# One more pass of count products in layers 1 to 3 of a graph network, and another placing of layer 0's chunk counts

## The reference

```python
edge_index = jnp.stack([src, dst])
# layer 0: hypercomplex message, gate and degree norm, summed at the destination
m = clifford_linear(h_src * r_uv, msg_w, msg_b) * gate * norm
h_out = clifford_linear(h_hc + segment_sum(m, dst), upd_w, upd_b)
x = _layernorm(x + h_out)
# layers 1 to 3: mean over the neighbours, two products
def _sage_conv(x, src, dst, Wl, bl, Wr, n):
    return _mean_aggregate(x, src, dst, n) @ Wl.T + bl + x @ Wr.T
h = relu(_sage_conv(x, src, dst, W1l, b1l, W1r, n))
h = relu(_sage_conv(h, src, dst, W2l, b2l, W2r, n))
x = _layernorm(x + _sage_conv(h, src, dst, W2l, b2l, W2r, n))
```

## Time and profile before

| | us |
|---|---|
| median of 3 runs | 3838.79 |
| lowest and highest run | 3831.48, 3844.26 |
| span of the profiled execution | 3293.7 |
| setup | about 170 |
| layer 0 | about 1397 |
| layers 1, 2, 3 | about 573, 570, 584 |

### The profile page before, as it was taken

How to read it: one execution, slowest core, us unless ns; L and a number is a source line. 1 busy time by engine, 2 the same in 40 slices (tenths; PEclk the granted TensorE clock), 3 DMA queues, 4 the chain that set the end, 5 groups by cost and what they waited for, 6 DMA issues and landing times. The chain is left out here.

```text
span 3293.7 us, 54777 instructions
## 1 busy us (share of the span) xinstructions
PE 2864.3 (87%) x16731; PEld 2464.3 (75%) x16731; DVE 2458.8 (75%) x5529; ACT 2224.0 (68%) x3945; POOL 2351.4 (71%) x2185
## 2 busy tenths in 40 slices
PE   6559999999999989997599999669999957999985
PEld 4448877787778878786488888558888846888884
DVE  7968888888888888887466667546666745787786
ACT  1057777777777777774577877468877836777771
POOL 6267777777777777773577777567777756777773
PEclk6579999999999999998799999889999978999997
DMA  4256666665556666663766666376666647666662
GB/s 136 73 133 168 173 165 167 167 167 165 167 164 168 165 173 167 168 169 113 228 196 201 199 194 188 105 246 207 201 195 197 184 134 225 204 210 205 206 185 89
DMA packets 335600, 573.59 MB, mean 174 GB/s; under 512 B 47029, under 2 KB 231686, under 8 KB 335302
## 3 DMA queue, kind: packets, MB, share of 16 engines
q0 software_dynamic: 101088, 277.97, 30.4%
q1 hardware_dynamic: 230697, 289.55, 28.1%
q10 hardware_dynamic: 3517, 2.48, 0.3%
HBM read 491.85 MB, written 77.97 MB: 173 GB/s over the span
## 5 line engine op out<-in xcount | busy, mean ns | idle before, releaser
L1483 POOL DMA_INDIRECT rows_arena<-table_h,src_idx x1128 | 1236.6, 1096 | 483.8 <-issue 364.0
L2052 PE MATMUL bank<-wide_counts,h_pairs 128*128 128x512 f32 (+1 forms) x4116 | 945.7, 384 | 123.6 <-ACT wide_counts L1632 104.0
L1483 POOL DMA_INDIRECT rows_arena<-table_scaled_x,src_idx x782 | 839.0, 1073 | 285.8 <-issue 273.6
L2052 PEld LDWEIGHTS bank<-wide_counts,h_pairs 128*128 128x128 f32 x4116 | 735.4, 193 | 262.9 <-issue 128.3
L1989 PE MATMUL bank<-rel_pairs,ftype_hot 125*128 125x258 f32 x4688 | 711.0, 299 | 51.3 <-ACT ftype_hot L1610 51.0
L1989 PEld LDWEIGHTS bank<-rel_pairs,ftype_hot 125*128 125x128 f32 x4688 | 620.6, 191 | 85.5 <-ACT ftype_hot L1610 51.1
L1632 ACT CAST wide_counts<-rows_arena 128x1024 fp32r<-128x1024 bf16 (+1 forms) x525 | 549.8, 1047 | 68.0 <-DMA rows_arena<-edge_counts 67.9
L1832 DVE TENSOR_TENSOR h_pairs<-rows_arena,h_pairs 128x512 fp32r<-128x512 f32 (+1 forms) x525 | 352.9, 682 | 259.6 <-ACT h_pairs L1629 254.9
L1824 DVE TENSOR_TENSOR row_pairs<-rows_arena,row_pairs 128x1024 fp32r<-128x1024 f32 x282 | 343.1, 1218 | 208.8 <-ACT row_pairs L1619 202.5
L1629 ACT CAST h_pairs<-rows_arena 128x512 fp32r<-128x512 f32 (+1 forms) x525 | 320.9, 611 | 197.3 <-PE bank L2052 152.9
L1653 ACT CAST rows_arena<-bank 128x448 bf16<-128x448 f32 (+1 forms) x812 | 368.3, 505 | 119.3 <-PE bank L2038 74.9
(11 more groups left out here) (186 smaller groups left out, 3098.9 us busy)
## 6 DMA issues: line engine op xcount, KB each, us to landing
rows_arena<-edge_counts SPq DMA_DIRECT2D x234, 512.0 KB, 4.0
edge_counts<-fcount SPq DMA_DIRECT2D x52, 832.0 KB, 6.3
rows_arena<-in_edge_type_dram SPq DMA_DIRECT2D x195, 187.5 KB
rows_arena<-table_h SPq DMA_DIRECT2D x36, 512.0 KB, 11.9
rows_arena<-table_h,src_idx POOLq DMA_INDIRECT x1128, 3.6
rows_arena<-table_scaled_x,src_idx POOLq DMA_INDIRECT x782
table_h<-chunk_info SPq DMA_DIRECT2D x96, 128.0 KB, 4.0
rows_arena<-edge_counts SPq DMA_DIRECT2D x39, 256.0 KB, 3.1
```

Of the source, the lines that this page charges most:

```text
L1483: pool.indirect_dma_start(out=rows[:, g % ring, c, :], out_offset=None, in_=table[:, :], in_offset=bass.IndirectOffsetOnAxis(ap=src_idx[:, ...
L2052: last = pe.matmul(bank[2 + h][:, 0:cols_of(w)], h_pairs[:, v % HALVES, part, b % HALF, h * P:(h + 1) * P], wide_counts[:, v % HALVES, b % ...
```

## The change

```diff
-PASSES, PASS_COLS, LAST_COLS = 7, 512, 256
+PASSES, PASS_COLS, LAST_COLS = 8, 512, 256
...
             def counts_at(position):
-                return [i for i in range(ND if first else 0) if i * 2 * NG // ND == position]
+                quad = [i for i in range(ND if first else 0) if i * NG // ND == position // 2]
+                return quad[-1:] if position % 2 else quad[:-1]
```

## The result

The kernel after took 3785.67 us (median of 4 runs, 3774.07 to 3796.82), the kernel before 3841.53 us on the same occasion (4 runs). The ratio is 0.9845, interval 0.9807 to 0.9884: the change makes the kernel faster by 1.5%. The prediction said slower, 4045 us.

What follows compares the result with a forecast made beforehand. The prediction took DVE to bound layer 0 and PE layers 1 to 3; 106 + 25 + 25 + 32 + 1 = 189 us on the 3293.7 us span became a 4045 us median, range 3930 to 4150 us.

Steps and rivals of the forecast that it cites:

- From the span to the median: Whole kernel: timed runs lie 545 us above the span; adding 189 us gives 4028 or 4059 us, middle 4045.
- The sum for the profiled execution: Whole kernel: 106 + 25 + 25 + 32 + 1 = 189 us, on a span of 3293.7 us.
- layers 1 and 2: The eighth pass adds 44.9 us on PE, sixteen quads less remove 16.5 us: +25 us for each layer.
- layer 3: The same +25 us, and seven node blocks moved to the end, -13 and +20 us: +32 us.
- Layer 0's term: 64 more counts at 1.52 us each on DVE, 97 us, and eight more clears, 9 us: +106 us.
- The placing: Layer 0: two products in a row in 78 quads, hidden in DVE's slot; rival that 40 to 90 us surface, 15 in 100.
- The signs: Profile after: DVE waiting tens of us for relation products means the placing shows; shorter layers 1 to 3 mean gathers led.
- PE as the bound of layers 1 to 3: PE is busy for 451.3 of 461 us in layer 1's main stretch, so added matmuls cost time there.
- The end of layer 3: 16 node blocks come after the last quad, where 9 did; DVE takes 2.91 us each, 20 us more.
- the gathers were the pace: Rival, layers 1 to 3: POOL's gathers set the pace, 90 us go from each layer, some 3660 us; 7 in 100.
- Its own threshold: The rival that gathers set the pace decides from the point where each of layers 1 to 3 gains over 35 us.
- The rule on weight loads: Layers 1 to 3: by the weight loads' busy share PE has 16% to spare, room for all 49 added units; not followed.

Runs made afterwards that it cites:

- experiment 1: The kernel before, unchanged, profiled anew on a pausing chip: 3785.52 us, span 3785.9 us.
- the first profile: The profiled execution of the kernel before that the prediction read: span 3293.7 us, with no pauses.
- experiment 2: The kernel after, unchanged, on the same pausing chip as experiment 1: 3736.01 us, ratio 0.9887 to the kernel before.
- experiment 9: The kernel after, unchanged, on a quiet chip: 3505.29 us against 3297.95 us for the kernel before, ratio 1.0621.
- experiment 3: Kernel before with layer 0 counting eight passes, layers 1 to 3 still seven passes and 94 quads: 3814.3 us, ratio 1.0069, pausing chip.
- experiment 6: Kernel before with eight passes of dense products in layers 1 to 3, still 94 quads: 3418.18 us, ratio 1.0379, quiet chip.
- experiment 7: Kernel before with only 78 of 94 quads in layers 1 to 3, still seven passes: 3239.97 us, ratio 0.9837, quiet chip.
- experiment 10: The kernel of experiment 6 again, beside the kernel before on another quiet chip: 3414.62 us, ratio 1.0342.
- experiment 17: Kernel before with two of four row gathers left out from the fifth quad on in all four layers: 3228.94 us, ratio 0.8555, pausing chip.
- experiment 15: Kernel before with plain transfers replacing two of four gathers from the fifth quad on in layers 1 to 3: 3534.24 us, ratio 0.9388, pausing chip.
- experiment 16: Kernel before with 18 short POOL clears replacing two of four gathers from each fifth-on quad, layers 1 to 3: 3513.72 us, ratio 0.9326, pausing chip.
- experiment 5: Kernel before with two of four gathers left out from the fifth quad on in layers 1 to 3: 3234.85 us, ratio 0.9822, quiet chip.
- experiment 12: The kernel of experiment 6 on a pausing chip: 3906.46 us, ratio 1.0142 to the kernel before.
- experiment 13: The kernel of experiment 7 on a pausing chip: 3646.29 us, ratio 0.9463 to the kernel before.
- experiment 11: The kernel of experiment 5 on a pausing chip: 3533.08 us, ratio 0.9161 to the kernel before.
- experiment 4: Kernel before with eight passes and 78 quads in layers 1 to 3, layer 0 still counting seven: 3686.85 us, ratio 0.9756, pausing chip.
- experiment 8: Kernel after with a wait and 60 PE register additions behind 17 quads in each of layers 1 to 3: 3520.53 us, ratio 1.0692, quiet chip.
- experiment 18: Kernel after with two of four row gathers left out from the fifth quad on in all four layers: 3466.58 us, ratio 0.9179, pausing chip.

## Why the prediction was wrong

- **"From the span to the median" failed.** The prediction saw that the timed runs lay 545 us above the span and carried its sum over in two ways, as a fixed part or as a factor of 1.166, with 4045 us in the middle. The runs showed that a gap of this size is pauses in layers 0 to 3, and that these answer to the change: on one pausing chip 490 us before (experiment 1, 492 us over the first profile's span) and 233 us after (experiment 2). It named the gap, built on the stages of an execution that had none of it, and took for granted that the change would leave it alone or stretch it. "No row says what that is" was right, and should have widened the range to a gain; it was 7 in 100.
- **The sum for the profiled execution was right.** 189 us forecast, 204 us in the windows of experiment 9, +207 us by its times. By terms: layer 0 106 forecast and 121 measured, layers 1 and 2 25 each and 16 and 19 measured, layer 3 32 and 48.
- **Layer 0's term.** On a quiet chip DVE sets the pace and each count costs it 1.9 us (121/64), a little over the 1.52 us and the clears. On a pausing chip DVE is busy for 71% of the layer (1195.54 of 1678), the pauses of PE set the pace, and the same counts cost 38 us (experiment 3).
- **The placing** was hidden, as said. PE now waits for ACT's staging 103 times and 114.7 us on the quiet chip, against 26.0, but DVE's waits for relation products grew to 5.6 us only. How much of the 15 us by which layer 0 exceeded its term is the placing isn't known. With seven passes the old and the new rule put all 406 counts in the same places, so the placing has no effect apart from the eighth pass. With 470 counts the old rule too would put three into 78 quads, 38 of them with two at the second place; it wasn't tried.
- **The signs** misled in the pausing condition. DVE waited for relation products by tens of us in the kernel after (68.0 us, and 61.2 "remote"), which was to mean that the placing shows; but the kernel before has 52.3 and 107.7 us of the same waits in experiment 1, with the old placing.
- **PE as the bound of layers 1 to 3** is shown for a quiet chip by experiments 6, 7 and 10: +126 and +117 us for a pass, -52 us for 16 quads. The end of layer 3 was undersized: with eight passes and 94 quads it takes 636 us (experiment 6), with 78 quads 637 us, so the quads taken away give nothing back there.
- **The rival "the gathers were the pace"** had the right instruction and the wrong mechanism. On a quiet chip POOL isn't the pace. On a pausing chip nothing waits for them for long either; PE's pauses come with them. Its own threshold (each layer gains over 35 us) was met in layer 2 only.
- **The rule on weight loads** (the Trainium skill, "Perfetto Trace Analysis", Identifying the Most-Contended Engine) would have given room for the pass. The quiet runs don't bear it out: the layer grew although PEld was busy for 452.79 of 582 us.

How the pauses go with the gathers, by windows of the same work on both kinds of chip (where the quiet side has no such run, experiment 17 takes layer 0 of before and experiments 15 and 16 take experiment 5). POOL's share is its busy time over the layer's, on the quiet chip where there is a run, else in the run itself:

| layer | gathers, per us on the quiet chip | POOL busy | quiet, pausing (us) | longer by |
|---|---|---|---|---|
| before, 0 | 978, 0.70 | 75% | 1397, 1678 | 20% |
| before, 1 | 376, 0.66 | 73% | 566, 627 | 11% |
| after, 0 | 978, 0.64 | 71% | 1518, 1715 | 13% |
| experiments 6 and 12, 1 | 376, 0.63 | 67% | 601, 659 | 10% |
| experiments 7 and 13, 1 | 312, 0.58 | 61% | 540, 567 | 5% |
| experiment 15, 1 | 196, 0.36 | 60% | 542, 552 | 2% |
| after, 1 | 312, 0.54 | 57% | 582, 596 | 2% |
| experiment 16, 1 | 196, 0.36 | 54% | 542, 544 | 0% |
| experiment 17, 0 (quiet: as before) | 596, 0.43 | 50% | 1397, 1393 | 0% |
| experiments 5 and 11, 1 | 196, 0.36 | 40% | 542, 546 | 1% |

The eighth pass takes 64 gathers out of each layer and makes the layer longer, and the counts make layer 0 longer for the same gathers; both lower the rate, and POOL's share with it. That one of the two is what matters is read from this table and not shown, and they aren't told apart: the loss follows POOL's share about as well as the rate. The rows come from several chips, and layer 3 of experiment 13 doesn't fit (623 us against 575, 8%, at 0.54 per us).

## What to carry to other kernels

Compare the span of the profiled execution with the timed runs before pricing anything on it: if they differ by more than the timed runs do among themselves, the profile may be of another condition, and the terms read from it may have the wrong sign. Price a change against both conditions where waits "remote" or clock falls show that there are two. In this kernel, on a pausing chip, trading gathers for matmuls won 89 us in layers 1 to 3 (experiment 4), though PE seldom waits for a gather and the same trade costs time on a quiet chip.

## What the runs showed of the hardware

- The same program takes 3292 to 3298 us on some chips and 3766 to 3852 us on others, with a spread of up to 1.4% between the runs on one chip. The records number the chips: 5 and 13 paused, 2 was quiet, and number 0 was quiet in experiments 5 to 8 and paused in 15 to 18. Whether that was one device in two conditions or two devices isn't known.
- On a pausing chip the engines that wait for PE are released several us late (228 "remote" waits in experiment 1, the longest 9.9 us), and PE itself starts matmuls late: it had 54 gaps of over 3 us in experiment 1 and 14 in the first profile. The other engines' instructions take as long as ever. Gathers bring this about: with half of them left out in all layers 546 us go, of which the same cut in layers 1 to 3 takes 57 us on a quiet chip too. Plain transfers of the same packets and bytes from the same queue don't (552 us against 546). Why a gather should hold PE up stays open.
- The recording is different on a pausing chip as well. The trace of experiment 1 holds 26,602 updates of semaphores and the first profile 58,163, for the same program. The lack is 31,600 there, and some of it comes without pauses: halving the gathers of layers 1 to 3 on a quiet chip takes 16 updates for each of 540 gathers (49,567 in experiment 5), so experiment 17, with 922 gathers less, should hold some 43,400; it holds 36,564 and has no pauses. (This also speaks against its chip having turned quiet by then.) Each timed run has a span and a granted clock on record, so no run tells what the kernel takes when nothing is recorded. That the recording has a part in the pauses wasn't tested and isn't excluded. The number of updates by itself doesn't bring them: experiment 15 raises as many as before.
- The clock falls behind the pauses. In experiment 1 it fell 90 times for 658 us in all, in the first profile 26 times for 254 us; 68 of the 90 falls come 0 to 5 us after a gap of PE of over 2 us has begun (counted from 180 us on), and so do 17 of the 26 in the first profile. The Trainium skill says that activity releases the throttle and that half clock is the idle state ("TensorE: Matmul & The Clock Gate", Part 1: The HAM clock gate); by that rule the falls are an effect of the pauses, and the order in the traces agrees. By the windows of layer 1 the fall costs PE 29 us of busy time (535.36 against 505.90), and the rest of the 61 us is stillness.
